# Three comparisons of a sparsemax threshold pass moved from VectorE to ScalarE

## The reference, cut to what matters

```python
def sparsemax(z):                               # over 32 patterns
    z_sorted = -jnp.sort(-z, axis=-1)
    cum = jnp.cumsum(z_sorted, axis=-1)
    support = 1.0 + k * z_sorted > cum
    k_sup = jnp.sum(support, axis=-1, keepdims=True)
    tau = (take(cum, k_sup - 1) - 1.0) / k_sup
    return jnp.maximum(z - tau, 0.0)

x = x + layernorm(attention_with_sparsemax(layernorm(x)))   # 16 heads, 32 key patterns
x = x + layernorm(ffn(layernorm(x)))   # slots, 16 experts (256 -> 1024 -> 256), second attention
```

## Time and profile before

| | |
|---|---|
| median of 3 runs | 469.0 us (467.04, 469.0, 472.23) |
| the profiled execution's own time | 470.11 us |
| its span | 468.3 us |
| TensorE busy (share of the span) | 392.9 us (84%) |
| VectorE busy | 311.2 us (66%) |
| ScalarE busy | 225.3 us (48%) |
| GpSimd busy | 146.9 us (31%) |

### The profile page before, as it was taken

The page is one execution under the profiler, slowest core; times in us unless marked ns, Lnnn a source line. Parts: engine busy times, 40 slices in busy tenths (PEclk is TensorE's granted clock), DMA queues, the critical chain, the costliest instruction groups (busy, mean ns, idle before and its releaser), DMA issues. The chain is left out here.

```text
span 468.3 us, 6940 instructions
## 1 busy us (share of the span) xinstructions
PE 392.9 (84%) x2071; PEld 244.3 (52%) x2075; DVE 311.2 (66%) x1189; ACT 225.3 (48%) x412; POOL 146.9 (31%) x243
## 2 busy tenths in 40 slices
PE   3886576678989959999999898989997669999983
PEld 3542232234545535655767756634443237888872
DVE  3689999998999985677515425334333124989996
ACT  2236558576677878778765643100000001356661
POOL 4104644755758432333032100010000000335353
PEclk9997978789989998999999999999999889999997
DMA  4284110010101045627828954969999999801215
GB/s 149 93 272 135 44 45 15 31 45 2 45 1 47 8 161 186 212 81 274 275 90 310 351 193 154 341 241 405 387 395 395 388 382 339 304 0 46 71 65 179
DMA packets 44318, 83.78 MB, mean 179 GB/s; under 512 B 1910, under 2 KB 36348, under 8 KB 39932
## 3 DMA queue, kind: packets, MB, share of 16 engines
q1 hardware_dynamic: 43224, 82.15, 49.7%
q10 hardware_dynamic: 1060, 1.22, 0.8%
HBM read 70.78 MB, written 12.58 MB: 178 GB/s over the span
## 5 line engine op out<-in xcount | busy, mean ns | idle before, releaser
L1097 PE MATMUL bank<-Wz,yT 128*128 128x512 f32 x128 | 70.9, 706 | 24.4 <-DVE top L1677 21.8
L1097 PEld LDWEIGHTS bank<-Wz,yT 128*128 128x128 f32 x128 | 28.3, 229 | 60.0 <-issue 46.4
L1677 DVE MAX8 top<-bank 128x8 f32<-128x32 f32 x512 | 51.5, 181 | 1.9 <-ACT arena L762 1.7
L1033 ACT ACTIVATE d<-d 128x32 f32<-128x32 f32 x16 | 3.7, 229 | 87.9 <-DVE d L2061 87.9
L1130 PE MATMUL bank<-aWo,hoT 128*128 128x256 f32 x128 | 37.9, 421 | 0.2 <-DVE arena L1823 0.2
L703 POOL TENSOR_TENSOR work<-work 128x512 f32<-128x512 f32 x16 | 16.6, 1059 | 65.9 <-DVE work L2136 65.9
L595 POOL TENSOR_SCALAR veps<-mv 128x4 f32<-128x4 f32 x24 | 5.9, 244 | 86.3 <-DVE mv L1605 61.7
L1193 PE MATMUL bank<-d,work 128*128 128x256 f32 x128 | 30.2, 381 | 1.6 <-ACT d L861 1.6
L1164 PE MATMUL bank<-arena,Wd 128*128 128x512 f32 x64 | 29.4, 599 | 1.5 <-ACT arena L833 1.5
L1537 PE MATMUL bank<-scr,work 128*128 128x256 f32 x128 | 29.1, 381 | 1.6 <-ACT work L1046 1.6
L1513 PE MATMUL bank<-scr,arena 128*128 128x256 f32 x128 | 28.9, 380 | 0.0
(11 more groups left out here) (274 smaller groups left out, 869.8 us busy)
## 6 DMA issues: line engine op xcount, KB each, us to landing
arena<-in_L_ffn_e_W_dram SPq DMA_DIRECT2D x14, 1024.0 KB, 11.5
scr<-in_L_ffn_e_W_dram SPq DMA_DIRECT2D x7, 1024.0 KB, 13.7
x<-in_L_ffn_e_W_dram SPq DMA_DIRECT2D x5, 1024.0 KB, 4.8
x<-in_L_ffn_e_Wg_dram SPq DMA_DIRECT2D x5, 1024.0 KB, 11.4
xin<-in_L_attn_query_dram SPq DMA_DIRECT2D x8, 512.0 KB, 4.0
x<-in_L_attn_query_dram SPq DMA_DIRECT2D x1, 4096.0 KB, 16.5
out_dram<-x SPq DMA_DIRECT2D x8, 512.0 KB, 4.2
away_dram<-arena SPq DMA_DIRECT2D x8, 512.0 KB, 8.9
```

Of the source, the lines that this page charges most:

```text
L1097: mm = pe.matmul(bZ[t % 2][:, :], yT[:, c, t * P:(t + 1) * P], Wz[:, c, :], start=(c == 0), stop=(c == C - 1))
L1677: mx = v.max(top[:, h * TG + t, :], bZ[t % 2][:, h * NS:(h + 1) * NS])
```

## The change

ScalarE's queue gets three more passes: `mark(4)`, `mark(5)` and `mark(6)`, each right behind the second half of the clamp of its group. VectorE loses the comparison at L1707 for groups 4, 5 and 6, and waits for the mark in its place. The rest of the diff is the bookkeeping of the semaphore counts.

```diff
             clamp(4, range(1, 2))
+            mark(4)
             take_a(2)
...
             clamp(5, range(1, 2))
+            mark(5)
             take_a(5)
             take_h(4)
...
             clamp(6, range(1, 2))
+            mark(6)
             take_a(9)
             take_h(8)
...
                 v.wait_ge(relued, i * 2 + 2)
                 v.tensor_reduce(exc[:, :], d3, AX_X, ALU.add).then_inc(newton, 1)
-                if marks:
-                    v.wait_ge(marked, i + 1)
-                else:
-                    v.wait_ge(signed, min(i, GB + 1))
-                    v.tensor_scalar(above[:, :], d[:, :], 0.0, None, ALU.is_gt).then_inc(newton, 1)
-                    v.wait_ge(newton, steps_ahead(i, b) + 2)
+                v.wait_ge(marked, i + 1)
                 fold_marks(i)
```

More of the change, by code:

```diff
@@ L1694, in scores_at, with steps_ahead, count @@
                 return scr[b][:, :, bass.ds(i * TG - b * KT, TG), :]
-            def steps_ahead(i, b):
-                return i * NW if b == 0 else GB * NW + (i - GB) * (NW + 1)
-            def count(i, b, marks):
+            def steps_ahead(i):
+                return i * NW
+            def count(i):
                 v.wait_ge(relued, i * 2 + 2)
                 v.tensor_reduce(exc[:, :], d3, AX_X, ALU.add).then_inc(newton, 1)
-                if marks:
-                    v.wait_ge(marked, i + 1)
-                else:
-                    v.wait_ge(signed, min(i, GB + 1))
-                    v.tensor_scalar(above[:, :], d[:, :], 0.0, None, ALU.is_gt).then_inc(newton, 1)
-                    v.wait_ge(newton, steps_ahead(i, b) + 2)
+                v.wait_ge(marked, i + 1)
                 fold_marks(i)
@@ L1734, in new_threshold, with settle @@
                 v.tensor_tensor(tauf[:, :], tau[:, :], rcnt[:, :], ALU.add).then_inc(tau_ready, 1)
-            def settle(i, b, marks, joined=-1):
-                new_threshold(i, steps_ahead(i, b) + (2 if marks else 3), joined)
+            def settle(i, b, joined=-1):
+                new_threshold(i, steps_ahead(i) + 2, joined)
                 v.tensor_reduce(tot[:, 0, bass.ds(i - b * GB, 1)], cnt[:, :], AX_X, ALU.add).then_inc(newton, 1)
@@ L1756, in finish_last @@
                 output_statistics(2)
-                v.wait_ge(marked, GB + 1)
+                v.wait_ge(marked, NG)
                 fold_marks(i)
-                new_threshold(i, steps_ahead(i, 1) + 3)
+                new_threshold(i, steps_ahead(i) + 3)
                 v.wait_ge(tau_ready, i + 1)
@@ L1770, in check @@
                 n = GB + b
-                v.wait_ge(newton, steps_ahead(GB * (b + 1) - 1, b) + NW + b)
+                v.wait_ge(newton, steps_ahead(GB * (b + 1) - 1) + NW + b)
                 v.wait_ge(signed, GB * (b + 1) + b)
@@ L1960, in batch_of_scores @@
                 sort_top(i + 1, range(2))
-                count(i, b, True)
-                settle(i, b, True)
+                count(i)
+                settle(i, b)
                 sort_top(i + 1, range(2, TG))
@@ L1980, in _ @@
                     output_statistics(g - 1)
-                count(i, 1, False)
-                settle(i, 1, False, g - 1)
+                count(i)
+                settle(i, 1, g - 1)
                 if g > 0:
```

## The result

The changed kernel takes 472.62 us in the median (470.03 to 475.41, 20 runs), the kernel before beside it 470.15 us (467.04 to 473.0, 20 runs). The ratio is 1.0046, 95% interval 1.0026 to 1.0066: 2.2 us slower, between 1.2 and 3.1. The forecast was 469.5 us where the median before was 469.0 (3 runs), so +0.5 us.

The account below looks back on a forecast made before the run. VectorE looked like the bound, but TensorE and ScalarE's chain at about 170 us was taken to decide. VectorE's terms summed to +0.82 us, ScalarE's shift of +0.49 ended the section: 469.0 to 469.5 us, range 466.0 to 473.0.

Parts of the forecast that it names:

- rival 1: ScalarE becomes the bound, marks exposed at `take_a(5)` and `take_h(8)`: 1.5 to 3.9 us slower, about 471.5; chance 25%.
- The walk: Following shifts through the engines' queues in groups 4 to 7, ending about 0.5 us later.
- Group 4, absorbed: The mark delays TensorE at most 1.0 us, taken up at ScalarE's wait; `signs(4)` stays at about 123.3.
- Group 5, clamp, +0.83: ScalarE regains 0.95 us at the clamp, the mark adds 1.94; `take_a(5)` goes from 130.74 to 131.57.
- Group 5, join, wait of 2.25 us, start at 138.40: VectorE's first join waits for late `norm_o(0)`, keeping 0.25 of its 2.50 us saved.
- Group 6: Clamp +0.49; the mark delays `norm_o(1)` to 160.02, so VectorE's second join puts it from -0.76 to +0.82.
- Group 7: ScalarE's clamp moves from 170.41 to 170.90; VectorE's first half, done at about 170.5, fits under it.
- Sum, +0.49 at the end of the section: VectorE nets +0.82, but ScalarE is the later one at 170 us, so its +0.49 decides.
- The clock, "I take no difference, since the idle time is the same": TensorE's low clock behind its stop before `mix(5)`: a slow stretch could cost or return 1.6 us; none counted.
- Rival 2, VectorE the bound: Marks hide in ScalarE's idle time and joins don't wait: 465.3 us, or 467.1 with half the gain; chance 17%.
- The sign `turn_a(16)`: TensorE's first instruction of the second batch entry: 2 us later means rival 1, 2 us earlier rival 2.

Follow-up runs that it names:

- e1: The kernel before with only group 4's comparison replaced by ScalarE's mark; ratio 0.9970 to before.
- e6: The changed kernel with TensorE's 2.50 us stop ahead of `mix(5)` filled with 11 unneeded matmuls; ratio 1.0000 to before.
- e9: The kernel before, unchanged, traced a second time; first flag to `take_h(12)` 66.40 us, against 66.41 in its first trace.
- e8: The changed kernel, unaltered, traced a second time; first flag to `take_h(12)` 68.55 us, against 67.14 in its first trace.
- e3: The kernel before with only group 6's comparison replaced by ScalarE's mark; ratio 1.0009 to before.
- e11: The kernel before with unneeded matmuls put in TensorE's stops ahead of `mix(4)` (7) and `mix(5)` (2); ratio 1.0018 to before.
- e2: The kernel before with only group 5's comparison replaced by ScalarE's mark; ratio 1.0094 to before.
- e5: The kernel before without comparison or mark in groups 4 to 6, so their thresholds are wrong; ratio 0.9956 to before.
- e4: The changed kernel with `mark(5)` moved behind `take_a(5)`, `take_h(4)` and `take_a(6)`; ratio 0.9960 to before.
- e12: The changed kernel with `mark(5)` three copies later, plus 12 unneeded matmuls in TensorE's stop ahead of `mix(13)`; ratio 0.9961 to before.

## Why the prediction was right, and where it was off

The range (466 to 473) held the time, 472.62, but only by 0.4 us, and with a part that had been put there for rival 1. The walk came out in most of its rows. The size did not: +0.5 was forecast, +2.2 (1.2 to 3.1) came. Of the 3.1 us between 469.5 and 472.62, 1.15 are the base (469.0 in 3 runs, 470.15 in 20) and 2.0 the change.

- *Group 4, absorbed*: right; `signs(4)` at 123.41 against "about 123.3". What I did not say is that group 4 by itself is a gain (e1, 1.25 us), which the mark of group 5 then spends.
- *Group 5, clamp, +0.83*: `take_a(5)` at 131.66 against 131.57, `mix(5)` at 132.66 against "about 132.6".
- *Group 5, join, wait of 2.25 us, start at 138.40*: wait 1.70, start 137.87. `norm_o(0)` is only 0.24 later, not 0.83, because `mix(5)` in this trace still ran at full clock (0.65 us in place of 1.09) and `project` took 1.94 us in place of 2.08, so ScalarE got its next tile sooner. In the second trace, where `mix(5)` was slow, the wait was 2.41.
- *Group 6*: clamp +0.69 against +0.49, second join at 160.32 against 160.05, wait 1.57 against 1.58.
- *Group 7*: clamp at 171.11 against 170.90, and VectorE's lateness did fit under ScalarE's.
- *Sum, +0.49 at the end of the section*: +0.73 in the trace in which the two kernels' stretches of low clock are about equally long (1.7 us missing in both). For that case the sum was right to 0.25 us, but in part by luck. The walk let TensorE carry the +0.83 of group 5 on to group 6, since it has no gaps up to 148 us. In e6 `mix(5)` is as late as in the changed kernel, and the section still ends 1.0 us earlier than before: at full clock TensorE has 1.29 us of wait for VectorE at 143 us, which the first trace did not show (e9). The scores that it waits with start 35.02 us behind the flag in e9, 35.16 in the first trace of before, 34.52 in e6 and 36.21 in the changed kernel. So the lateness came through with the low clock, and did not without it.
- *The clock, "I take no difference, since the idle time is the same"*: this is the term that failed. Idle time was nearly the same, but its effect was not. The stop of 2.5 us was followed by 1.7 and 3.4 us of missing clock (after, e8), the stops of 1.77 and 0.72 us by 1.7, 0 and 1.7 (before, e9, e3); these are too few traces to say that the first kind loses more. What the runs do show is that the price of a missing us differs: nothing in the kernel before (e9, e11), where VectorE arrived later at 143 us anyway; most of it in the changed one, where VectorE is earlier and TensorE sets the end of the section (after, e8 and e6). With full clock in both, the change would gain 1.0 us in the section (e6); with what the stop brings, it loses 0.7 to 2.1.
- *Rival 1, marks exposed, +1.5 to +3.9*: the timed +2.2 lies in its bounds, but its mechanism is not what happened in the changed kernel. The clamp's wait was given back as walked, and the joins waited about as forecast. It names the right place, though: e2, with no gain from group 4 to pay with, is this rival (`mix(5)` 1.95 us later, +2.3 us in the section, +4.4 timed).
- *Rival 2, VectorE the bound*: fell. 43.78 of 45 us busy did not make its 3.75 us worth 3.75: free of all table work the kernel gains 2.1 us (e5). Yet it was not all wrong for the kernel before: there VectorE was the later one at 143 us, which the first trace hid behind the low clock.
- *The sign `turn_a(16)`*: it decided nothing. Counted from the first flag it starts 0.3 us earlier in the changed kernel's first trace than in the first of before, and 2.2 us later in the second (e8 against e9). The low clock behind the stop ahead of `mix(13)` lies in front of it, and the changed kernel's first trace had none there.

What stays open: the 2 us by which e2's timed loss exceeds its trace, and whether a stop's length sets the length of the low clock behind it. The longest low clock at 132 (3.4 us missing) came behind the stops of 2.5 and 2.66 us (e8, e2), but the changed kernel's first trace had 1.7 behind the same stop, and behind the one at 263 us came either 1.7 us or nothing.

## What to carry to other kernels

Before a pass is moved to an engine with idle time, look at what stands behind the place where it is put, and let the copies for which another engine is already waiting go first: the same 1.9-us pass three copies later turned a loss of 2.2 us into a gain of 1.9. Don't subtract a stretch of low clock, or add one, until you know who else arrives at its end; a second trace of the unchanged kernel shows what is fixed in it and what is chance. Compare short sections between fixed marks: the 20 timed executions of each kernel here scatter by 5 to 6 us.

## What the runs showed of the hardware

- The low clock behind one and the same stop varies from execution to execution, from 0 (after, e1, e6) over about 1.7 (before, e2, e3, e5) and 3.4 (e8 to e11) to 5.1 us (e4) of full clock missing behind the stop of about 3 us ahead of `mix(13)`, costing 0 to 2 us.
- Even a stop of 1.35 us was followed by low clock in 3 of the 14 traces (after, e1, e6): eight matmuls took 3.52 us in one and 2.00 in another.
- With a stop filled with 9 to 12 matmuls of 128x512 bf16, the clock behind it was 1.00 in the one trace of each of e6, e11 and e12. It was 1.00 without a fill too in e9, and behind the stop ahead of `mix(13)` in after, e1 and e6, so single traces do not prove the fill. The timed runs gained about 2 us by it in e6, where TensorE sets the end of the section, and nothing in e11 and e12.
